# Three places for the weighted values of attention a, weights in three pairs of PSUM banks, and the second half's first softmax pass ahead of all rounds

## The reference

```python
mask = jnp.asarray(_log_sparse_mask(Lx))      # j = i and j = i - 2**k
raw = jnp.einsum('blhd,bmhd->bhlm', q, k)      # 16 heads of width 8
scores = jnp.where(mask, raw, 0.0) / scale     # masked entries are 0, not -inf
attn = jax.nn.softmax(scores, axis=-1)
out = jnp.einsum('bhlm,bmhd->blhd', attn, v)
return out @ Wo.T + bo
```

## Time and profile before

| | us |
|---|---|
| median of 3 runs | 607.86 (606.92 to 613.08) |
| the profiled execution's own time | 608.75 |
| its span in the profile | 606.9 |
| TensorE, VectorE, POOL, ScalarE busy in the span | 469.4, 381.7, 239.2, 225.0 |
| granted TensorE clock, mean over the span | 0.879 of full |
| first `expand` starts, last `residual_a` ends | 50.69, 119.33 |

### The profile page before, as it was taken

The page is one execution under the profiler, slowest core; times in us unless marked ns, Lnnn a source line. Parts: engine busy times, 40 slices in busy tenths (PEclk is TensorE's granted clock), DMA queues, the critical chain, the costliest instruction groups (busy, mean ns, idle before and its releaser), DMA issues.

```text
span 606.9 us, 10872 instructions
## 1 busy us (share of the span) xinstructions
PE 469.4 (77%) x3458; PEld 365.2 (60%) x3458; DVE 381.7 (63%) x1097; ACT 225.0 (37%) x815; POOL 239.2 (39%) x249
## 2 busy tenths in 40 slices
PE   2954756553399809999999999999999975708993
PEld 1411434442399806778787778778787854608993
DVE  7898564496166635776767576775767555834662
ACT  1500000041144403664646466563656361404441
POOL 6102524447244522443434343344424342461543
PEclk9967678955599958999999999999999998557997
DMA  8999300002356320000000000000000000126560
GB/s 288 411 421 422 155 0 0 1 1 97 115 162 191 113 69 2 2 1 2 1 0 0 0 0 0 0 0 0 0 0 0 1 1 2 35 105 180 149 190 20
DMA packets 22004, 47.57 MB, mean 78 GB/s; under 512 B 3249, under 2 KB 13623, under 8 KB 19537
## 3 DMA queue, kind: packets, MB, share of 16 engines
q1 hardware_dynamic: 18960, 40.79, 19.5%
q0 software_dynamic: 3008, 6.34, 3.1%
HBM read 23.88 MB, written 24.15 MB: 79 GB/s over the span
## 4 chain that ended last, share of the span: by engine, by line
issue 61%; PE 18%; DVE 7%; POOL 6%; DMA 3%; SPq 1%; ACT 1%; POOLq 0%; ACTq 0%; DVEq 0%
PE ps L788 7%; PE ps L801 6%; POOL sum L438 3%; PE ps L643 2%; DVE prod L978 2%; POOL sum L442 2%; POOL sorted_in L462 1%; DMA woa<-in_wo_a 1%; DMA pv<-in_w 1%; PE ps L778 1%; DMA pv<-sorted_in 1%; PE ps L671 1%; PE ps L730 1%; DVE pv L1016 1%; DVE stat L1080 1%
## 5 line engine op out<-in xcount | busy, mean ns | idle before, releaser
L497 POOL TENSOR_TENSOR vT<-vT,prec 128x256 f32<-128x256 f32 (+1 forms) x128 | 103.0, 824 | 168.6 <-DVE prec L1286 168.6
L604 ACT ACTIVATE vT<-ps,nmax 128x128 f32<-128x128 f32 (+1 forms) x256 | 104.9, 433 | 26.3 <-DVE nmax L1278 26.3
L612 ACT COPY prod<-ps 128x384 f32<-128x384 f32 x96 | 42.9, 481 | 117.9 <-PE ps L888 114.3
L1278 DVE TENSOR_REDUCE nmax<-ps 128x2 f32<-128x256 f32 (+1 forms) x128 | 62.4, 550 | 33.9 <-PE ps L868 33.9
L833 PE MATMUL ps<-xnT,wb 128*128 128x256 f32 x256 | 67.2, 385 | 4.6 <-DVE xnT L1258 3.9
L888 PEld LDWEIGHTS ps<-cst,vT 128*128 128x128 f32 x384 | 44.7, 141 | 18.7 <-issue 15.8
L604 ACT ACTIVATION_READ_ACCUMULATOR vT<-ps,nmax 128x1 f32 x256 | 55.9, 218 | 0.0
L888 PE MATMUL ps<-cst,vT 128*128 128x128 f32 x384 | 52.5, 273 | 1.8 <-POOL vT L497 1.7
L901 PE MATMUL ps<-prod 128*64 128x256 f32 (+1 forms) x512 | 48.7, 331 | 3.0 <-ACT prod L612 2.1
L862 PE MATMUL ps<-qk 64*128 64x128 f32 (+1 forms) x512 | 51.0, 338 | 0.0
L833 PEld LDWEIGHTS ps<-xnT,wb 128*128 128x128 f32 x256 | 44.5, 194 | 10.6 <-DVE xnT L1258 4.3
(11 more groups left out here) (148 smaller groups left out, 837.2 us busy)
## 6 DMA issues: line engine op xcount, KB each, us to landing
sorted_in<-zero SPq DMA_DIRECT2D x1, 16512.0 KB, 59.0
pv<-in_w SPq DMA_DIRECT2D x30, 259.0 KB
pv<-sorted_in SPq DMA_DIRECT2D x46, 129.0 KB
wps<-in_w SPq DMA_DIRECT2D x1, 2072.0 KB, 9.8
w2s<-in_w SPq DMA_DIRECT2D x1, 2048.0 KB, 14.0
wb<-in_w_b SPq DMA_DIRECT2D x1, 1536.0 KB, 18.1
xres<-in_x SPq DMA_DIRECT2D x4, 256.0 KB, 3.6
xres<-after_ffn SPq DMA_DIRECT2D x4, 256.0 KB, 3.7
```

Source lines behind the costliest of these rows:

```text
L497: last = nc.gpsimd.tensor_tensor(px, px, view(prec, m_at(n, x) + t * 2, [[1, 2], [0, (t + 1) * P]]), ALU.mult)
L604: last = nc.scalar.activation(pb[:, o:o + (t + 1) * P], wide[:, c:c + (t + 1) * P], ACT.Exp, bias=nmax[:, m:m + 1], accum_out=psum[:, m:m ...
L612: nc.scalar.copy(pT[:, c:c + BLOCKS * P], bank[hh][:, 0:BLOCKS * P]).then_inc(b_pa, 1)
L1278: last = nc.vector.tensor_reduce(nmax[:, m:m + 2], view(wide, x * 1024 + t * P, [[512, 2], [1, (t + 1) * P]]), AX.X, ALU.max, negate=True)
```

## The change

- `pv` and `sum2` get three places (`RP = 3`) in place of two. The first step of a round waits for `out_a(r - 3)` instead of `out_a(r - 2)`, and so does the second addition of POOL.
- `pv` grows from 5160 to 7680 columns. `xsT` and `ys`, which had tensors of their own, now lie in `pv` from column 5160 on.
- `expand` goes round three pairs of banks (4 and 5, 6 and 7, 2 and 3) and waits until step i - 3 has been weighed. Since the second half's scores lie in banks 2 and 3, `expand(2)` also waits for `less_max(1)`.
- `less_max(1)` moves from behind round 0 to ahead of it on VectorE. `weights(1)` stays behind round 2.
- `out_a((i - 8) // 3)` is issued behind `expand(i)` for i = 8, 11, 14, ..., that is behind the third step of a round instead of the second.
- `o_bank` alternates between banks 0 and 1 every two rounds, and the first `out_a` of each pair of rounds waits for the `residual_a` two pairs before it.

```diff
+RP = 3
+XS_AT = WR * WP + XR * ROW + 2 * F
-        pv = sb("pv", [P, 2 * 2 * SLOTS * P + 5 * NE])
+        pv = sb("pv", [P, RP * 2 * SLOTS * P])
-        sum2 = sb("sum2", [P, 2 * 2 * 2 * P])
+        sum2 = sb("sum2", [P, RP * 2 * 2 * P])
-        xsT = [sb(f"xsT{i}", [P, P]) for i in range(2)]
+        xsT = [pv[:, XS_AT + i * P:XS_AT + (i + 1) * P] for i in range(2)]
-        ys = [sb(f"ys{i}", [P, D]) for i in range(YR)]
+        ys = [pv[:, XS_AT + (2 + i) * P:XS_AT + (3 + i) * P] for i in range(YR)]
         def e_bank(i):
-            return (4 + i % 2 * 2) * 512
+            return (4, 6, 2)[i % 3] * 512
         def o_bank(r):
-            return (r // 2 - 1 if r >= ROUNDS else 0) * 512
+            return r // 2 % 2 * 512
# POOL, add_up
-                need(pool, a_y, r - 1)
+                need(pool, a_y, r - RP + 1)
# TensorE, expand
-                need(pe, a_pv, i - 1)
+                need(pe, a_pv, i - 2)
+                if i == 2:
+                    pe.wait_ge(a_lm, 2)
# TensorE, out_a
-                if r == 2:
-                    pe.wait_ge(a_x, 1)
+                if k % 2 == 0:
+                    need(pe, a_x, r // 2 - 1)
# TensorE, the order
-            expand(0)
-            expand(1)
-            for i in range(2, 3 * NR):
+            for i in range(3 * NR):
                 expand(i)
-                if i >= 7 and i % 3 == 1:
-                    out_a((i - 7) // 3)
+                if i >= 8 and i % 3 == 2:
+                    out_a((i - 8) // 3)
# VectorE, weigh_values
-                    need(dve, a_y, r - 1)
+                    need(dve, a_y, r - RP + 1)
# VectorE, the order
             weights(0)
+            less_max(1)
             for r in range(NR):
                 for c in range(3):
                     weigh_values(3 * r + c)
-                if r == 0:
-                    less_max(1)
```

More of the change, by code:

```diff
@@ L436, in add_up @@
                 need(pool, a_sum, r)
-                o = r % 2 * 2 * SLOTS * P
+                o = r % RP * 2 * SLOTS * P
                 own.after(nc.gpsimd.tensor_tensor(view(sum4, 0, [[4 * P, 2], [1, 4 * P]]),
@@ L440, in add_up @@
                                                   view(pv, o + 4 * P, [[SLOTS * P, 2], [1, 4 * P]]), ALU.add))
-                need(pool, a_y, r - 1)
-                nc.gpsimd.tensor_tensor(view(sum2, r % 2 * 4 * P, [[2 * P, 2], [1, 2 * P]]),
+                need(pool, a_y, r - RP + 1)
+                nc.gpsimd.tensor_tensor(view(sum2, r % RP * 4 * P, [[2 * P, 2], [1, 2 * P]]),
                                         view(sum4, 0, [[4 * P, 2], [1, 2 * P]]),
@@ L678, in out_a @@
                 pe.wait_ge(a_pv, 3 * r + 3)
-                if r == 2:
-                    pe.wait_ge(a_x, 1)
+                if k % 2 == 0:
+                    need(pe, a_x, r // 2 - 1)
                 for j in range(2):
                     o = o_bank(r) + (2 * k + j) % 4 * P
-                    slots = [sum2[:, (r % 2 * 2 + j) * 2 * P + s * P:(r % 2 * 2 + j) * 2 * P + (s + 1) * P] for s in range(2)]
+                    q = (r % RP * 2 + j) * 2 * P
+                    slots = [sum2[:, q + s * P:q + (s + 1) * P] for s in range(2)]
                     for s in range(8, rest(t) + 1):
-                        c = (r % 2 * 2 + j) * SLOTS * P + s * P
+                        c = (r % RP * 2 + j) * SLOTS * P + s * P
                         slots.append(pv[:, c:c + P])
@@ L1010, in weigh_values @@
                 if c == 0:
-                    need(dve, a_y, r - 1)
+                    need(dve, a_y, r - RP + 1)
                 for s in (4 * c, 4 * c + 2) if c < 2 else range(8, rest(t) + 1):
-                    o, w = r % 2 * 2 * SLOTS * P + s * P, e_bank(i) + (s - 4 * c) * P
+                    o, w = r % RP * 2 * SLOTS * P + s * P, e_bank(i) + (s - 4 * c) * P
                     if c < 2:
```

## The result

The changed kernel takes 585.46 us (median of 4 runs, 583.89 to 587.35), the kernel before 609.09 beside it (4 runs, 606.92 to 613.08). The ratio is 0.961, with a 95% interval of 0.957 to 0.965: 23.6 us less. The profiled execution's span is 584.6 us, against 606.9.

The account below looks back on a forecast made before the run. Rounds bound by waits, chiefly VectorE's products for out_a. New end: weights(1) to 70.4, then 71.8, plus 22.2 of TensorE to 94.0, 0.5 and 0.8 to 95.3, 2.5 clock to 97.8; 21.5 less gives 586.5, range 581 to 597.

Parts of the forecast that it names:

- The place: VectorE's products wait 23.3 us for out_a; with three places 3 us or less of that wait remains.
- The start and rounds 0 to 2: On VectorE: less_max(1) 3.0 us to 53.6, three rounds 8.4 us to 62.0, expand(2)'s new wait costing nothing.
- `weights(1)`: On VectorE behind round 2: 8.4 us, 62.0 to 70.4, still colliding with POOL's sums; 6.3 without collision, 10.7 with one more.
- TensorE behind it: From 71.8 us TensorE bounds: 22.2 us of expansions and out_a, 4.76 us a second-half round, to 94.0.
- The wait for POOL at the end: Last out_a waits 0.5 us: products and POOL's sums take 5.3 us beside 4.8 us of matmuls.
- Behind the stage: After the rounds everything keeps its old length; 1.5 us either way allowed for the clock.
- The sum: The rounds' last residual_a ends at 97.8 instead of 119.33, 21.5 us less; time to expect 586.5.
- the spell: TensorE at 1.2 GHz behind weights(1), over two steps and most of an out_a: 2.5 us.
- A: Rival on TensorE: clock stays at 1.2 GHz throughout, gain 1.7 us, time 606; more spells 591 to 594; chance 0.08.
- B: Rival in the rounds: VectorE's products and POOL's sums shut each other out, gain 4, time 604; chance 0.04.
- C: Rival: 46 expert slots each pay 0.98 us for ys and xsT in pv, slower, time 631; chance 0.03.
- D: Rival: VectorE waits as long elsewhere, as for expansions behind an out_a; gain 2 us, time 606; chance 0.03.

Follow-up runs that it names:

- p1: Kernel before with only three places in pv and sum2 and the move of xsT and ys: stage 52.5 us, ratio to before 0.982 (0.969 to 0.995).
- p2: Changed kernel with two places again, three bank pairs and early first pass kept: stage 58.2 us, ratio to before 0.990 (0.985 to 0.995).
- w2: Changed kernel with five needless matmuls in TensorE's wait during weights(1): stage 43.4 us, ratio to before 0.963 (0.958 to 0.967).
- c1: Changed kernel with POOL's sums of round 2 held until weights(1) is done: stage 43.7 us, ratio to before 0.964 (0.959 to 0.969).
- p3: Kernel before with only less_max(1) moved ahead of the rounds: stage 62.4 us, ratio to before 0.994 (0.989 to 0.999).
- w1: Changed kernel with eight needless matmuls in TensorE's wait during weights(1): stage 44.6 us, ratio to before 0.964 (0.959 to 0.969).
- o2: Changed kernel with out_a(2) issued right behind out_a(1), ahead of expand(12): stage 43.4 us, ratio to before 0.961 (0.957 to 0.966).

## Why the prediction was right, point by point

**The place.** The wait of products for `out_a` held the rounds, and the third place ends it. p1 and p2 show it from both sides. What p1 adds is that the place alone would have stopped at the next wait, 8 us short; the prediction took places and banks in one step and did not say how they share.

**The start and rounds 0 to 2.** `less_max(1)` took 3.0 us as said (49.91 to 52.92), the three rounds 8.2 for 8.4, and the new wait of `expand(2)` cost nothing. The stage began 0.55 us earlier than before. The change had no part in that: two more profiles of the same kernel begin it at 51.67 and 49.28 us.

**`weights(1)`.** 8.4 forecast, 8.1 measured, and for the reason given, though in other places: the subtraction stood 0.6 us, and the small L1004 stood 1.26 for POOL's next sum.

**TensorE behind it.** The bound was right and its size too large. I had 4.76 us to a round in the second half; it is 4.34. The busy time of a group includes the end of its last matmul, which lies under the start of the next group. So the 1.99 + 0.70 us that I added are one group of 2.42, followed 2.34 later, and 2.07 of `out_a` count as 1.9 to 2.0 where the next group follows. Over all that TensorE still had to do that is 1.9 us. Round 4's expansions and `out_a` took 1.7 us more than round 5's in this profile and 2.9 in another, for 2.5 forecast; by w2's rows 0.3 of that belongs to starting behind a wait and not to the clock. The wait for POOL at the end was 1.30 us instead of 0.5, by the same oversize: the products and sums behind `expand(22)` took 5.4 us, as said, but the matmuls beside them 4.2 instead of 4.8.

**Behind the stage.** I allowed 1.5 us and 2.5 were lost in this profile, 2.4 of them to a fall of the clock in attention b that two other profiles of the same kernel don't have.

**The sum.** 97.8 was forecast for the stage's end, 94.53 came: 1.3 us from all before round 4, 1.9 from the groups, 0.8 from the spell, less 0.8 for POOL. 586.5 against 585.46 is closer than the parts were, and that is luck: the stage gained 3.3 us more than the sum said, and 2.5 were lost behind it. (587.2 less the 0.9 of that execution is also 586.3, not 586.5.)

**The rivals.** A fell: the grant of the stage rose from 0.82 to 0.92, with one spell behind the low start. The Trainium skill's rule of a clock that swings where a kernel cycles through PSUM banks ("TensorE: Matmul & The Clock Gate", the section on psum-queue depth-cycling) did not show here, with three pairs of banks and a grant of 1.00 from 75 us on. B fell: the 32 large products took 676 to 692 ns although POOL's sums ran beside most of them. What does stand for POOL are instructions with both operands in SBUF (1.55 against 0.29 us, c1). That agrees with the Trainium skill ("SBUF — State Buffer", section "Who interferes with whom"), by which two SBUF inputs on VectorE contend with a GpSimd instruction that reads SBUF and one does not. C fell: the way from the stage's end to attention b, with 23 expert slots in it, took 106.1 to 109.9 us in the kernels with the moved buffers, and 108.7 and 107.8 in the two without (before and p3). D fell with p1, in which the waits for `out_a` went and 11.3 us of others came, and the stage was 16.1 us shorter all the same.

## What to carry to other kernels

When an engine waits for a buffer to come free, look for the wait that stands behind it before counting the gain: here a third buffer alone gave 16 us, the banks and the early pass another 8, and behind TensorE, POOL was next by only half a microsecond a round. A pass that must be done anyway belongs where the other engines are still filling, and work that is ready belongs in the long wait of its engine: here it cost nothing as long as it ended before the wait did, and the clock stayed up behind it. Price a pipelined engine by the distance from one group's start to the next group's, not by the groups' busy times.

## What the runs showed of the hardware

TensorE's low spell behind 4.9 to 5.0 us of idle time cost 1.4 us in one execution of a kernel and 2.6 in another; it came behind 3.56 us too (c1). With needless matmuls (w1, w2), or with useful ones (o2), in the idle time the profiles show none. Two fp32 matmuls of 64 rows by 512 columns on different halves of the rows take 1.0 us together (an expansion), and 0.87 us each when they use the same half one after the other. The same addition of 1024 columns takes 2.35 us on POOL and 1.22 on VectorE.
